# Graph network on one Trainium2 core: diagonal sum made in columns, centred projection, features product after the second adjacency product

## What is computed

```python
def _L0_gnn_ref(h, node_adj, edge_adj, ...):
    ...
    edge_output = _gru_cell(node_support, h, edge_Wih, edge_Whh, edge_bih, edge_bhh)
    ...
    node_output = _gru_cell(edge_support, h, node_Wih, node_Whh, node_bih, node_bhh)
    return de[:, None] * edge_output + dn[:, None] * node_output

def _L1_gnn_ref(h, adj, simlar, W_proj, b_proj, W_gcn, b_gcn):
    ...
    h2 = jnp.tanh(h @ W_proj + b_proj)
    feat = jax.nn.relu(new_adj @ (h2 @ W_gcn) + b_gcn)
    return feat

x = _layernorm(x + _L0_gnn_ref(x, adj, adj, ...), axis=-1)
x = _layernorm(x + _L1_gnn_ref(x, adj, adj, ...), axis=-1)
```

## Time and profile before

| | |
|---|---|
| runs | 1318.92 us median of 3 (1317.95 to 1318.94) |
| the profiled execution | 1318.72 us, span 1317.1 us |
| PE busy | 1304.8 us (99%) |
| DVE busy | 1009.5 us (77%) |
| ACT busy | 936.3 us (71%) |
| POOL busy | 102.5 us (8%) |
| third stage, from the first gate to the first graph product | 981.31 to 1081.87 us |
| from there to the last product | 1081.87 to 1312.10 us |

### The profile page before, as it was taken

The page is one execution under the profiler, slowest core; times in us unless marked ns, Lnnn a source line. Parts: engine busy times, 40 slices in busy tenths (PEclk is TensorE's granted clock), DMA queues, the critical chain, the costliest instruction groups (busy, mean ns, idle before and its releaser), DMA issues.

```text
span 1317.1 us, 12199 instructions
## 1 busy us (share of the span) xinstructions
PE 1304.8 (99%) x4203; PEld 590.0 (45%) x4203; DVE 1009.5 (77%) x1427; ACT 936.3 (71%) x950; POOL 102.5 (8%) x188
## 2 busy tenths in 40 slices
PE   8999999999999999999999999999999999999998
PEld 3444444444444444444444444444444555444445
DVE  2433333457998998999989999899868988678885
ACT  4655555338988899889889899898945556545563
POOL 0100001000100100100100100100003562000000
PEclk9999999999999999999999999999999999999999
DMA  9988888263233242232323423322113437888880
GB/s 367 355 291 287 281 296 295 79 238 127 84 139 130 95 146 96 97 143 97 145 99 116 152 96 122 118 96 96 64 62 129 144 115 252 296 307 294 302 285 18
DMA packets 46712, 228.95 MB, mean 174 GB/s; under 512 B 10611, under 2 KB 16436, under 8 KB 21044
## 3 DMA queue, kind: packets, MB, share of 16 engines
q1 hardware_dynamic: 44082, 225.55, 48.6%
q10 hardware_dynamic: 2562, 2.56, 0.6%
HBM read 223.80 MB, written 4.29 MB: 173 GB/s over the span
## 4 chain that ended last, share of the span: by engine, by line
PE 96%; DMA 2%; DVE 1%; issue 0%; SPq 0%; POOL 0%; ACT 0%; POOLq 0%
PE t_y_ps L1821 49%; PE ns_ps L427 15%; PE t_y_ps L1374 13%; PE rows_ps L1374 4%; PE t_y_ps L1799 3%; PE t_y_ps L1313 3%; PE t_y_ps L1315 2%; DMA pieces<-in_adj_c 2%; PE t_es_ps L1788 2%; PE pos_ps L441 1%; PE rows_ps L1315 1%; PE t_y_ps L1371 1%; PE t_es_ps L1346 1%; PE t_y_ps L1339 1%; DVE mask L1737 0%
## 5 line engine op out<-in xcount | busy, mean ns | idle before, releaser
L1821 PE MATMUL t_y_ps<-mask,x_sb 128*128 128x512 f32 x1536 | 662.6, 592 | 0.2 <-DVE mask L1737 0.2
L1821 PEld LDWEIGHTS t_y_ps<-mask,x_sb 128*128 128x128 f32 x1536 | 290.6, 190 | 366.0 <-issue 350.0
L1737 DVE TENSOR_TENSOR mask<-mask 128x1536 f32<-128x1536 f32 x256 | 450.1, 1759 | 0.2 <-ACT mask L1621 0.2
L1621 ACT ACTIVATE mask<-mask,ones 128x1536 f32<-128x1536 f32 x256 | 399.7, 1562 | 0.0
L1614 ACT ACTIVATE mask<-mask,pieces 128x512 f32<-128x512 f32 x352 | 241.5, 712 | 35.0 <-PE t_y_ps L1821 32.8
L427 PE MATMUL ns_ps<-pieces,x_sb 128*128 128x512 f32 x504 | 226.5, 602 | 6.8 <-DMA pieces<-in_adj_c 6.6
L1723 DVE TENSOR_SCALAR mask<-mask,e_cols 128x512 f32<-128x512 f32 x416 | 189.0, 487 | 50.6 <-PE t_y_ps L1821 44.2
L1115 ACT ACTIVATE mask<-mask 128x2048 f32<-128x2048 f32 x64 | 121.7, 1909 | 80.5 <-DVE mask L1226 80.0
L1374 PE MATMUL t_y_ps<-mask 128*128 128x512 f32 x384 | 167.0, 592 | 0.1
L427 PEld LDWEIGHTS ns_ps<-pieces,x_sb 128*128 128x128 f32 x504 | 93.8, 192 | 123.0 <-issue 116.6
L291 DVE TENSOR_SCALAR mask<-pieces 128x2048 fp8e4<-128x2048 f32 x64 | 76.8, 1224 | 93.1 <-DMA pieces<-in_adj_c 75.2
(11 more groups left out here) (177 smaller groups left out, 614.5 us busy)
## 6 DMA issues: line engine op xcount, KB each, us to landing
mask<-in_adj_c SPq DMA_DIRECT2D x128, 1024.0 KB, 4.8
pieces<-in_adj_c SPq DMA_DIRECT2D x63, 1024.0 KB, 5.0
mask<-scratch_shifts SPq DMA_DIRECT2D x8, 1536.0 KB, 7.3
x_sb<-in_x_p SPq DMA_DIRECT2D x8, 256.0 KB, 9.9
mask<-in_x_t SPq DMA_DIRECT2D x1, 2048.0 KB, 16.8
pieces<-in_x_t SPq DMA_DIRECT2D x8, 256.0 KB, 3.0
pieces<-scratch_ns_t SPq DMA_DIRECT2D x8, 256.0 KB, 3.6
scratch_ns_t<-ns_sb ACTq DMA_DIRECT2D x7, 256.0 KB, 5.9
```

Of the source, the lines that this page charges most:

```text
L1621: nc.scalar.activation(t, t, ACT.Exp, bias=ones[:, :], scale=-1.0).then_inc(exped, 1)
L1737: nc.vector.tensor_tensor(term(n), term(n), a, ALU.mult).then_inc(terms, 1)
L1821: mm = nc.tensor.matmul(y_ps[c % 2][h][:, :], x_sb[:, k, :], term(n)[:, h, :], start=k == 0, stop=k == NB - 1)
```

## The change

- The diagonal is loaded as a row, broadcast to all partitions, 512 entries per chunk (`load_diag`), and DVE makes cells * diagonal + x in columns: `make_y` has three 512-wide operations, the last one signals `cells`. ACT copies the turned rows into x (`copy_rows`) and `measure` waits for that. The diagonal's gather at the start of the second stage goes. SP now waits for the last scaling of the second stage, and issues two diagonal loads, before the first pieces.
- Mean and projection are exchanged: PE makes W_proj minus its column means once (`center_weights`, one product after unit (5, 10) of the second stage, copied by ACT with `keep_center` after its own unit (5, 10)). `project` multiplies the columns of y by it, in four 128-wide products that give rows. DVE scales by the inverse root and adds b_proj (`scale_h`), ACT applies tanh straight into the features (`make_h2`). The transposes of x, their copy, `features` and its copy go. `finish_x` (the normalizing) moves behind the first graph products.
- W_gcn comes after the adjacency: `take_out` copies a finished chunk, `feed` multiplies it by W_gcn in 128-wide products instead of the transposes, and DVE adds the bias and then takes the maximum with zero and adds x. The last row tile has the same form as the others (copy, then one product), with its bias put into the bank first.

The core of the diff, without names and semaphores that only follow:

```diff
...
+    def load_diag(sp, c):
+        sp.dma_start(diag_rows[c % 2], dram["diag"][c * CW:(c + 1) * CW].partition_broadcast(P)).then_inc(diag_loaded[c % 2], 16)
...
+    def center_weights(pe, bank):
+
+        pe.wait_ge(w_loaded, 16 * WEIGHT_LOADS)
+        pe.wait_ge(bias_step, 10)
+        nc.tensor.matmul(bank[:, 0:H], center, w_proj, start=True, stop=True).then_inc(centered, 1)
+
+    def keep_center(act, bank):
+        act.wait_ge(centered, 1)
+        nc.scalar.copy(w_center, bank[:, 0:H]).then_inc(center_out, 1)
...
+        def copy_rows(c):
+            act.wait_ge(turned, c + 1)
+            nc.scalar.copy(x1[:, rows(c), :].rearrange("p r f -> p (r f)"), cell_ps[c % 2][:, :]).then_inc(rows_copied, 1)
...
             make_n("edge", c)
             read_hid("node", c)
+            if c:
+                copy_rows(c - 1)
             read_r("node", c)
             if c >= 2:
-                copy_x(c - 2)
+                make_h2(c - 2)
...
+            nc.vector.tensor_tensor(both, cell["edge"], cell["node"], ALU.add).then_inc(y_step, 1)
+            dve.wait_ge(y_step, 2 * c + 1)
+            dve.wait_ge(diag_loaded[c % 2], 16 * (c // 2 + 1))
+            nc.vector.tensor_tensor(both, both, diag_rows[c % 2], ALU.mult).then_inc(y_step, 1)
+            dve.wait_ge(y_step, 2 * c + 2)
+            nc.vector.tensor_tensor(both, both, x_t[c % 2], ALU.add).then_inc(cells, 1)
+
+        def scale_h(c):
+            dve.wait_ge(rooted, POOL_STEPS * (c + 1))
+            dve.wait_ge(projected, c + 1)
...
             pre_n("edge", c)
             if c >= 2:
-                finish_x(c - 2)
+                scale_h(c - 2)
             if c:
-                make_y(c - 1)
-                measure(rows(c - 1), stats, moments, stats_made, averaged)
+                measure_y(c - 1)
             make_cell("edge", c)
...
         for u in range(NPIECE, NPIECES):
             square_a(u)
             c, g = divmod(u, NPIECE)
+            if g == 3:
+                finish_x(c - 1)
+            if c == end and g == 6:
+                finish_x(end)
             if c < end and g == 5:
                 add_x1(c - 1)
...
+                mm = nc.tensor.matmul(h_ps[c % 2][:, q * P:(q + 1) * P], both[:, q * P:(q + 1) * P], w_center, start=True, stop=True)
+            mm.then_inc(projected, 1)
...
+                mm = nc.tensor.matmul(back_ps[i % 2][:, t * P:(t + 1) * P], feat_t[i % 2][:, t * P:(t + 1) * P], w_gcn,
+                                      start=i not in BIAS_FIRST, stop=True)
+            mm.then_inc(fed, 1)
...
             sp.wait_ge(terms_used, NB * NCHUNK)
-            sp.wait_ge(y_scaled, HEADS * (NCHUNK - 1))
+            sp.wait_ge(y_scaled, HEADS * NCHUNK)
+            for c in range(2):
+                load_diag(sp, c)
             sync_tail(sp)
...
+                if (c, k) == CENTER_AT:
+                    keep_center(act, rows_ps)
...
+                    if (c, k) == CENTER_AT:
+                        pe.wait_ge(shifts_out, NGROUP)
+                        center_weights(pe, rows_ps)
```

More of the change, by code:

```diff
@@ L1229, in add_x1 @@
             tiles, (c, q, end) = part_rows(i), END_PARTS[i]
[L1230 to L1237, removed]
+            n, source = end - q, back_ps[i % 2][:, q * P:end * P].rearrange("p (r f) -> p r f", f=H)
+            dve.wait_ge(fed, i + 1)
+            dve.wait_ge(x_done, tiles.stop)
+            if i not in BIAS_FIRST:
+                out = with_bias[:, 0:n * H].rearrange("p (r f) -> p r f", f=H)
+                nc.vector.tensor_tensor(out, source, b_gcn.unsqueeze(1).broadcast_to([P, n, H]), ALU.add).then_inc(y2_step, 1)
+                dve.wait_ge(y2_step, i + 1)
+                source = out
+            nc.vector.scalar_tensor_tensor(x1[:, tiles, :], source, 0.0, x1[:, tiles, :], ALU.max, ALU.add).then_inc(y2_done, 1)
             dve.wait_ge(y2_done, i + 1)
@@ L1277, in vector_tail @@
             make_cell("node", c)
-            add_cells(c)
+            make_y(c)
         end = NCHUNK - 1
-        finish_x(end - 1)
+        scale_h(end - 1)
         square_a(3)
-        make_y(end)
-        measure(rows(end), stats, moments, stats_made, averaged)
+        measure_y(end)
         square_a(4)
         square_a(5)
-        finish_x(end)
+        scale_h(end)
         for u in range(6, NPIECE):
@@ L1403, in tensor_tail @@
             gate("node", "r", c)
-            if c >= 2:
-                turn_x(c - 2)
+            if c == 1:
+                pe.wait_ge(center_out, 1)
+                pe.wait_ge(es_out, NCHUNK)
+            if c >= 1:
+                project(c - 1)
             gate("node", "z", c)
             gate("node", "in_n", c)
-            if c >= 3:
-                features(c - 3)
         end = NCHUNK - 1
-        project(end - 2)
         graph(0, 0)
@@ L1414, in tensor_tail @@
         turn_cells(end)
-        turn_x(end - 1)
-        features(end - 2)
-        graph(2, 0)
-        project(end - 1)
-        graph(3, 0)
-        features(end - 1)
-        graph(4, 0)
-        turn_x(end)
-        graph(5, 0, tiles=range(0, 2))
         project(end)
-        graph(5, 0, tiles=range(2, PIECE))
-        features(end)
-        end = (NCHUNK - 1) * NPIECE
-        for u in range(6, end):
+        for u in range(2, end * NPIECE):
             c, g = divmod(u, NPIECE)
@@ L1431, in tensor_tail @@
             if c and g == 2:
-                turn_features(c - 1)
-        for u in range(end, NPIECES):
-            graph(u, NCHUNK - 1, 0, CHUNK - 1)
-            if u == end + 4:
-                turn_features(NCHUNK - 2)
-        for u in range(end, NPIECES):
-            graph(u, NCHUNK, CHUNK - 1, CHUNK)
-            if u == end + 1:
-                turn_features(NCHUNK - 1)
-    return load_weights, load_in, make_biases, sync_tail, pool_tail, scalar_tail, vector_tail, tensor_tail
+                feed(c - 1)
+        last = len(END_PARTS) - 1
+        for u in range(end * NPIECE, NPIECES):
+            graph(u, end, 0, CHUNK - 1)
+            if u == end * NPIECE + 4:
+                feed(end - 1)
+        bias_first(last)
+        for u in range(end * NPIECE, NPIECES):
+            graph(u, last, CHUNK - 1, CHUNK)
+            if u == end * NPIECE + 1:
+                feed(end)
+        feed(last)
+    return load_weights, load_in, load_diag, make_biases, center_weights, keep_center, sync_tail, pool_tail, scalar_tail, vector_tail, tensor_tail
 def on_dve(k):
@@ L2600, in host_layout @@
         "adj": adj,
+        "diag": np.diagonal(adj),
         "adj_t": adj.reshape(NB, P, NB, P).transpose(0, 3, 2, 1).reshape(NB, P, N),
```

168 lines of the change are left out of this document (68 added, 100 removed).

## The result

The changed kernel takes **1350.58 us** (median of 5 runs, 1345.07 to 1350.95) against 1317.95 (1316.91 to 1318.94): ratio **1.0236**, 95% interval 1.0224 to 1.0247. It is slower, as forecast, but by 32.6 us instead of 19.5, and above the range (1332 to 1344). The profiled execution is the fastest of the five: 1345.07, span 1343.8, 26.7 more than the span before.

What follows compares the result with a forecast made beforehand. PE was taken as the bound before, DVE as setting the gates' period after. Terms 5.3 + 8.9 - 4.4 + 2.9 + 3.5 + 2.5 + 0.8 gave +19.5, 1338.2 us (chance 0.5), range 1332 to 1344.

Steps and rivals of the forecast that it cites:

- Rival (a): PE stays the bound: its 6.5 us are gained and 0.7 paid at the end, 1312.9 us; chance 0.05.
- Term 1: Centring the weight, second stage: ACT's copy must wait for PE's product, PE stands 5.1 us and works 0.2; +5.3.
- rival (b): Centring is hidden: ACT keeps a lead through it, 5.1 us less, 1333.1 us; chance 0.1.
- Term 2: Start of third stage: diagonal loads delay the first piece, DVE wins back about 2 us; first cells +2.7 us.
- Term 3: Gates: DVE sets the period, 12.8 us or 15.0 with a square; first graph +8.9 us against before.
- term 4: First graph units: -4.4 us for removed PE work, +2.9 for stalls of 0.9 and 2.0.
- Terms 5 to 7: Respectively: steady graph chunks +3.5 us from feed; last chunk +2.5 from PE's wait; end +0.8 for a copy and product.
- Rival (c): PE's clock falls in the 5.1 us centring gap, its products running at half clock; 1340.8 us; chance 0.25.
- Rival (d): POOL's root is late in each chunk, 1 us too much in six chunks; 1344.2 us; chance 0.1.

Runs made afterwards that it cites:

- e3: Changed kernel plus 17 unused 512-wide products on PE at six of its waits; 1341.35 us.
- e7: As e3, but make_y leaves out the multiplication with the diagonal, and chunks 3 and 5 have two unused products instead of three; 1335.28 us.
- e2: Changed kernel with only ACT's copy of the centred weight moved, from behind its unit (5, 10) to behind (5, 14); 1342.03 us.
- e5: Kernel before plus only the centring product behind PE's unit (5, 10) and ACT's copy behind its unit (5, 11); 1321.27 us, ratio 1.0022.
- e6: As e3, but SP issues the first three pieces before the two diagonal loads; 1337.98 us.
- e1: The changed kernel timed once more, nothing edited; 1348.89 us.
- e8: Changed kernel with copy at (5, 14), pieces before diagonals, unused products among gates and before graph unit 3, finish_x moved out of last graph chunk; 1332.17 us.

## Why the prediction was wrong

Split by places of the program, with the spans of the profiled executions (changed kernel, and e3 where the clock never falls):

| stretch | forecast | changed | e3 |
|---|---|---|---|
| launch and first stage | 0 | -1.5 | +0.5 |
| from `combine` of chunk 4 to the first gate | +5.3 | +7.7 | +5.4 |
| first gate to the first `cells` | +2.7 | +4.8 | +5.1 |
| first `cells` to the first `graph` | +6.2 | +7.8 | +6.2 |
| first `graph` to PE's last product | +5.3 | +7.8 | +6.1 |

The second line is 748.07 to 987.53 against 749.56 to 981.31, the next ones follow from 1009.86, 1100.67 and 1338.69 against 998.87, 1081.87 and 1312.10.

**The bound** was read rightly: DVE's 11.63 and its 1.3 us of room decided, not its 77% of the span. e7 confirms it. Rival (a), that PE stays the bound, is out.

**Term 1, centring, +5.3**: right in mechanism and size (4.84 and 0.2; e3 has +5.4 for the stretch). e2 and e5 show that it is ACT's lost lead: the wait is gone with four units of it and 1.99 in all with one. So rival (b) is out too.

**Term 2, start of the third stage, +2.7**: mechanism right, size wrong, 4.8 measured. The step that failed is "with the diagonals' own bytes the first piece lands some 3.3 us later". Counted from the first gate, the square starts 5.0 later (10.01 instead of 4.98): the issue is 2.9 later, as forecast, but the landing takes 2.1 longer instead of 0.4. The other 0.4 us are in what DVE was to win back: before, it had waited 0.72 and 0.93 for gates, 1.65 instead of 2. In e6 the order alone is worth 3.4. Why loads of 0.5 MB delay the piece behind them by so much, no run shows.

**Term 3, gates, and term 4**: right. 12.84 and 15.04 against 12.8 and 15.0, a wait of 0.80 against 0.8 for `copy_rows`, `graph` stalls of 1.00 and 2.22 against 0.9 and 2.0. In e3 the gates take exactly the forecast 6.2.

**Terms 5 to 7**: the `feed` stall is 2.37 against 2.5, and 0.35 stands at the end. The stretch took +6.1 in e3, 0.8 more than forecast. The unused products are not in it: from the first `graph` to unit 6 PE takes 25.65 in e3 and 25.62 in the changed kernel. About 0.6 lies before the first `feed` (0.3 of it in the two stalls of term 4), and 0.2 behind `feed(6)`.

**Rival (c), the clock**, is the step that cost the range: the sum has no term for it, and it is the larger of the two failures. Without any fall, e3's 1341.35 lies inside the range. The rival's mechanism held, and its price for the one gap, 2.6 us, was nearly what the windows show (2.4). The Trainium skill (TensorE: Matmul & The Clock Gate, What's actually happening) says that the clock falls back when PE idles, and the trace agrees (0.50 behind the wait of 4.84). Two things were wrong. It stood at 0.25, as if the fall were doubtful. "No row shows a wait of 5 us behind work at full clock" was not so: the trace of the kernel before has one at its end, 5 us of idle PE behind its last product and then a clock of 0.54. And it was asked at the 5.1 us gap alone, although my own terms 2, 3, 4 and 6 put waits of some 2 to 3 us on PE in five more places, each of which had to pass the same question. The profiled execution paid at two of these, 1.6 in the period of 14.41 and 1.7 in the graph stage. The other executions of the changed kernel, at a mean clock of 0.991, were 5.5 us longer than that one at 0.995. They have no trace of their own; e1 shows where such time can go (two falls more), and e3 that without falls it is gone. Forecast 19.5, plus 2.1 for the start of the third stage, plus 2.4 + 1.6 + 1.7 for the falls, less the 1.5 us that this execution gained before the centring, is 25.8 of the 26.7 measured; the 0.8 of terms 4 to 7 are nearly the rest.

**Rival (d)**, a late root, did not come: DVE waits 3.80 for it once, behind the gates, as before.

## What to carry to other kernels

Here a wait of PE of 2.2 us or more was not priced by its length: the products behind it could run at half clock, for up to 1.7 us lost each time and 2.4 at the gap of 4.84. So once a change makes PE wait, list every wait that the forecast itself implies and price each twice, without and with the fall. Where the wait can't be removed, unused products that are shorter than it cost next to nothing and here gave back 7.5 us; a wait that has become shorter needs fewer (e6). And an engine that stands idle once per period can still lose time in full, when another engine needs its result in the middle of the period (DVE's 1.62 above). And ahead of the first transfer that an engine waits for, put nothing that is not needed sooner: two loads of 256 KB in front of 1 MB cost 3.4 us, though their own reader came only 18.7 us after their issue (1008.45 less 989.76).

## What the runs showed of the hardware

Which waits brought the clock down, in the three profiles that have them:

| PE's wait | changed | e1 | e2 |
|---|---|---|---|
| 4.84, centring | fell | fell | no wait |
| 2.62, first cells | stayed | fell | fell |
| 3.18, chunk 3 | stayed | fell | fell |
| 3.18, chunk 5 | fell | fell | fell |
| 2.22, `graph` unit 6 | fell | fell | fell |
| 2.36, `feed(6)` | stayed | stayed | fell |
| 1.1 and less | stayed | stayed | stayed |

I had not expected a fall behind 2.2 us, nor that it can begin after the wait is over: PE resumed at 1126.29, and the clock read 0.92 over the window up to 1128 and 0.50 from there. Nine of the thirteen falls in the table began so, 0.9 to 1.5 us after PE resumed; only those of the centring and of chunk 3 began inside the wait. e3's wait of 1.76 and e8's of 1.73 brought none, and no run has a wait between these and 2.2. What decides for one and the same wait in different executions, these runs leave open.

The launch itself is a gap in the record: its first weight loads take 0.34 and the later ones 0.19, and yet the granted clock reads 1.00 there:

```profile
8.00:10.00 2.00, 2.00 (x4) 0.77 (x3) 1.23 (x1) 0.00 (x0) 0.00 (x0) 1.00 0.94 369
```

That those first products ran at half clock is thus read from durations alone.
